# GpSimd normalises the next chunk's x before it begins the result's sum: two yacc buffers, and first gates asked for one pair later

## The reference, cut to what matters

```python
xn = layernorm(x)                                   # x: [2, 2048, 128]
# 1. a selective state space layer with N = 16 states per channel
dt = soft_clamp(softplus(xn @ Wdt.T + bdt), 0.001, 0.1, 0.5)
B, C = xn @ WB.T, xn @ WC.T                         # [b, l, 16] each
dA = exp(soft_clamp(dt * A, -8, 8, 0.5))
h = dA[t] * h + dt[t] * B[t] * xn[t]                # for every t, rescaled if its norm is over 20
y = sum_n h[:, n] * C[t, n] + Dp * xn[t]
# 2. a mixture of 64 experts (top 8 within the best 4 of 8 groups) and a shared expert
g = gates(xn @ router_w.T)                          # [tokens, 64], most of them 0
routed = sum_e g[:, e] * (relu(xn @ up[e])**2 @ down[e])
shared = relu(xn @ shared_up)**2 @ shared_down
out = x + y + routed + shared
```

## Time and profile before

| what | value |
|---|---|
| median of 3 runs | 568.28 us (566.95 to 568.99) |
| the profiled execution's own time | 569.49 us |
| its span in the profile | 567.7 us |
| busy share of the span | PE 90%, DVE 86%, ACT 83%, POOL 83% |
| TensorE clock, mean of the span | 0.994 of full |
| DMA | 149.32 MB, mean 263 GB/s |

### The profile page before, as it was taken

One profiled execution on the slowest core, in us unless ns is written; L12 is line 12 of the kernel. 1 busy time (PEld: TensorE's weight loads), 2 busy tenths in 40 slices (PEclk: granted clock), 3 DMA queues, 4 the chain that ended last, 5 costly groups with the idle time before them and its releaser, 6 DMA issues.

```text
span 567.7 us, 7918 instructions
## 1 busy us (share of the span) xinstructions
PE 508.1 (90%) x1666; PEld 279.1 (49%) x1666; DVE 485.4 (86%) x1150; ACT 468.6 (83%) x922; POOL 472.4 (83%) x438
## 2 busy tenths in 40 slices
PE   2148999999999989999999999989999999999996
PEld 1025545464555545555455545545455554555552
DVE  3647899889988899889998889889998899979993
ACT  2767799798987989888986999869998789978872
POOL 2399889897998979897998978989898979979762
PEclk9998999999999999999999999999999999999998
DMA  8946877897869877697678877697777976789951
GB/s 202 326 163 227 272 250 228 282 321 248 268 201 359 267 260 255 235 383 253 241 251 314 302 261 259 195 365 269 268 248 236 360 254 238 236 331 351 321 183 38
DMA packets 65649, 149.32 MB, mean 263 GB/s; under 512 B 14048, under 2 KB 31040, under 8 KB 65600
## 3 DMA queue, kind: packets, MB, share of 16 engines
q1 hardware_dynamic: 63728, 147.07, 77.0%
q10 hardware_dynamic: 1872, 1.75, 0.9%
HBM read 143.03 MB, written 5.77 MB: 262 GB/s over the span
## 4 chain that ended last, share of the span: by engine, by line
POOL 44%; issue 26%; PE 14%; DVE 13%; DMA 2%; POOLq 1%; ACT 0%; SPq 0%; DVEq 0%; ACTq 0%
POOL yacc L549 15%; POOL bc_rows L540 9%; PE DN L1087 7%; POOL xn L446 3%; DVE g L834 3%; DVE relu L884 3%; DVE bc_rows L896 2%; PE U L1037 2%; PE U L1038 2%; PE U L1039 2%; DVE DC L943 2%; POOL xt L453 2%; POOL rstd L440 1%; DMA bc_rows<-bc_dram 1%; POOL ot L521 1%
## 5 line engine op out<-in xcount | busy, mean ns | idle before, releaser
L1087 PE MATMUL DN<-act,down 128*128 128x512 f32 x512 | 262.3, 594 | 1.8 <-ACT act L718 1.8
L884 DVE SCALAR_TENSOR_TENSOR relu<-U,gate_rows 128x512 f32<-128x512 f32 x256 | 173.7, 678 | 36.2 <-PE U L1039 18.3
L718 ACT ACTIVATE act<-relu 128x512 f32<-128x512 f32 x272 | 169.1, 622 | 37.4 <-DVE relu L884 31.9
L549 POOL TENSOR_TENSOR yacc<-yacc,bc_rows 128x512 f32<-128x512 f32 x120 | 153.8, 1282 | 43.5 <-DVE bc_rows L896 43.5
L1037 PE MATMUL U<-x_hi,up_hi 128*128 128x512 f32 x256 | 164.0, 641 | 15.3 <-DVE relu L884 13.6
L540 POOL TENSOR_TENSOR bc_rows<-dtx_all,bc_rows 128x512 f32<-128x512 f32 x128 | 164.6, 1286 | 13.5 <-DMA bc_rows<-bc_dram 13.5
L943 DVE TENSOR_TENSOR_SCAN DC<-DC,carry,bc_rows 128x512 f32<-128x512 f32 x96 | 122.7, 1278 | 0.0
L1087 PEld LDWEIGHTS DN<-act,down 128*128 128x128 f32 x512 | 95.6, 189 | 28.8 <-ACT act L718 6.5
L1038 PE MATMUL U<-x_lo,up_hi 128*128 128x512 f32 x256 | 101.4, 396 | 0.0
L1039 PE MATMUL U<-x_hi,up_lo 128*128 128x512 f32 x256 | 101.0, 394 | 0.0
L1037 PEld LDWEIGHTS U<-x_hi,up_hi 128*128 128x128 f32 x256 | 48.3, 188 | 103.5 <-DVE relu L884 61.0
(11 more groups left out here) (113 smaller groups left out, 495.1 us busy)
## 6 DMA issues: line engine op xcount, KB each, us to landing
bc_rows<-bc_dram SPq DMA_DIRECT2D x128, 512.0 KB, 5.9
gate_rows<-gate_dram SPq DMA_DIRECT2D x128, 512.0 KB, 4.8
xs<-in_L_attn_x SPq DMA_DIRECT2D x8, 256.0 KB, 5.2
down<-in_L_ffn_down_w SPq DMA_DIRECT2D x8, 256.0 KB, 4.9
xr<-in_L_attn_x SPq DMA_DIRECT2D x8, 256.0 KB, 6.4
rest_kept_dram<-rest SPq DMA_DIRECT2D x8, 256.0 KB, 4.4
out<-res SPq DMA_DIRECT2D x8, 256.0 KB, 4.5
dtx_all<-in_L_ffn_up_w SPq DMA_DIRECT2D x3, 512.0 KB, 5.4
```

What stands on the lines that cost most here:

```text
L549: g.tensor_tensor(yacc[:, :], yacc[:, :], c_rows[:, (c * N + n) % BUFS, :], ALU.add).then_inc(yacc_done, 1)
L718: a.activation(act_at(c, slot), relu[:, slot % 2, :], ACT.Square).then_inc(sq_done, 1)
L884: v.scalar_tensor_tensor(out=relu[:, slot % 2, :], in0=U[slot % 2][:, :], scalar=0.0, in1=gate_rows[:, k // 2 % SBUFS, slot % 2, :], op0=A ...
L1087: mm(DN[:, :], w, act_at(c, slot), start=slot == 0, stop=slot == SLOTS - 1).then_inc(down_done, 1)
```

## The change

POOL takes the power and the normalised x one slot earlier (slots 0 and 1 where they were in 1 and 2). `out_begin` moves from slot 0 to slot 5. So that the next chunk may start its sum before the old one is read, `yacc` gets two halves, used by turns, and the first `ymul` of a chunk waits for the `out_begin` of two chunks ago. In SP's list each gate row stands one state later.

```diff
-        yacc = sb("yacc", [P, CT])
+        yacc = sb("yacc", [P, 2, CT])
...
                     rows(c, n)
-                    if n:
-                        gates_in(c, n - 1)
+                    if n > 1:
+                        gates_in(c, n - 2)
+                gates_in(c, N - 2)
                 gates_in(c, N - 1)
...
             def prep(pc, slot):
                 chain = chains["p"]
-                if slot == 1:
+                if slot == 0:
                     pool.wait_ge(var_ready, pc + 1)
...
-                if slot == 2 and pc:
+                if slot == 1 and pc:
                     pool.wait_ge(rstd_ready, pc + 1)
...
-                g.tensor_tensor(ot[:, :], rest[:, par(c)], yacc[:, :], ALU.add).then_inc(ot_begun, 1)
+                g.tensor_tensor(ot[:, :], rest[:, par(c)], yacc[:, c % 2, :], ALU.add).then_inc(ot_begun, 1)
...
-                    g.tensor_tensor(yacc[:, :], yacc[:, :], c_rows[:, (c * N + n) % BUFS, :], ALU.add).then_inc(yacc_done, 1)
+                    g.tensor_tensor(yacc[:, c % 2, :], yacc[:, c % 2, :], c_rows[:, (c * N + n) % BUFS, :], ALU.add).then_inc(yacc_done, 1)
...
                 for slot in range(SLOTS):
-                    if slot == 0 and not first:
+                    if slot == 5 and not first:
                         out_begin(c - 1)
...
                 if n == 0:
-                    wait(dve, ot_begun, c)
-                dst = c_rows[:, (c * N + n) % BUFS, :] if n else yacc[:, :]
+                    wait(dve, ot_begun, c - 1)
+                dst = c_rows[:, (c * N + n) % BUFS, :] if n else yacc[:, c % 2, :]
```

## The result

| | before | changed |
|---|---|---|
| median in one comparison | 568.63 us (566.95 to 569.59, 4 runs) | 561.07 us (560.99 to 561.15, 4 runs) |
| profiled execution's own time | 569.49 us | 560.99 us |
| span | 567.7 us | 559.2 us |

The ratio is 0.987 (95%: 0.9854 to 0.9885). The medians are 7.6 us apart; by the interval the gain lies between 6.5 and 8.3 us. The profiled executions are 8.5 apart, because the profiled one of the kernel before is 0.9 above the median. The forecast was 560.1, with -8.2. The spread shrank too, from 2.6 us to 0.2.

The account below looks back on a forecast made before the run. PE and DVE were taken to bound the kernel as a pair, neither catching up a stall. PE's `xn` stalls in chunks 1 to 6 (7.2 shown plus 0.96) gave -8.2, chunk 0 gave 0: 568.28 to 560.1 us, range 557 to 565.

Parts of the forecast that it names:

- POOL's order: POOL at a chunk's start: power waits 0.53 us for the variance, yet `xn` is done 2.46 us earlier, 1.67 before PE needs it.
- SP's order: SP's load queue: row 2 issued at 228.1 instead of 233.4, 5.3 us earlier, so POOL's 1.16 us wait for it goes.
- both parts are needed for the whole 2.46: At chunk starts: `xn` comes the full 2.46 us earlier only with POOL's new order and SP's new list together.
- it is what allows `ot` to be late: Two halves of `yacc`: worth nothing by themselves, but they let POOL do `ot` behind the first sum.
- the boundaries each 1.2 to 1.6 us closer together: Sign expected in the profile after: every chunk boundary closer to the next by this amount.
- Does DVE follow?: DVE after the transposes: its waits, at least 0.94 us, cover PE's 0.85 gain, so DVE starts its own stage earlier by that.
- rival 1: DVE's stage absorbs half: only its `x_lo` wait, 0.39 of 0.85, is regained; gain 3.8 us, 564.5 us; chance 0.18.
- rival 2: No change: PE is early at slot 4 and waits for DVE's relu instead; 568 us; chance 0.10.
- Chunk 0: PE's longest stall, 2.30 us, counted as 0 gain because DVE waits 1.60 us for POOL there; upper bound 2.5.
- rival 4: More gain: chunk 0 pays too, up to 2.5 us; 557.6 us; chance 0.08.
- The rule that speaks against it: DMA queues take turns, so row 2 may delay the gate store by 1.9 us, leaving gate row 0 0.3 us spare, not 2.2.
- Rival 3: Slower: gate row 0 comes later than its 2.19 us slack at seven boundaries and DVE stands still; +17, 585 us; chance 0.06.

Follow-up runs that it names:

- sp_only: Kernel before with only SP's new list, each gate row one state later: 560.82 us, ratio 0.9877.
- power_and_sp: Kernel before with power and `xn` one slot earlier and SP's new list, but one `yacc` and `ot` in slot 0: 561.10 us, ratio 0.9849.
- pool_only: Changed kernel with SP's old list, so POOL's new order and two halves of `yacc` only: 561.70 us, ratio 0.9893.
- power_early_only: Kernel before with only the power in slot 0 and `xn` in slot 1; one `yacc`, SP's old list: 561.31 us, ratio 0.9883.
- ot_late_only: Kernel before with only two halves of `yacc` and `ot` in slot 5: 570.79 us, ratio 1.0057.
- The split runs: Changed kernel with POOL's chunk 0 weight splittings moved to DVE: the first, 559.11 us; the first two, 561.44; those two with POOL held for the second, 557.99.
- the limits in batch 2: Changed kernel with gate rows four or five states after their own state's row, 581.44 and 669.30 us; or with `xn` in slot 4 behind the sum, 589.11.
- split_two_held: Changed kernel with the first two chunk 0 weight splittings on DVE and POOL waiting for the second before `xt`: 557.99 us, ratio 0.9792.
- split_two_on_dve: Changed kernel with the first two of POOL's three chunk 0 weight splittings done by DVE: 561.44 us, ratio 0.9857.

## Why the prediction was right, by its own steps

**The size.** -8.2 us forecast, -8.5 between the profiled executions, -7.6 between the medians. The kernel before scatters by 2.6 us here and by up to 6.4 in the batches; sp_only and power_and_sp, whose own times are 560.8 and 561.1, read as gains of 7.1 and 8.3 against it. So the medians do not tell 7.2 from 8.2. The chunks do: the rule that a stall is counted from the distance of the records' starts (0.86), and not from the idle time shown, gave 0.16 per chunk, and the gains of the table lie 0.14 to 0.22 us above the idle times shown in five of six chunks (0.38 in the sixth).

**POOL's order.** The new wait for the variance was forecast at 0.53 us for each boundary and is 0.76 at chunk 1, 0.7 on average: the path from DVE's aggregation to POOL's next start costs more than the end of its record says. It lies in the slack. That is 1.5 us at chunk 1. At the start of chunk 3, for which 1.67 was forecast, it is only 0.84 (`xn` done at 240.96, PE's transposes at 241.80), for a reason that the prediction does not have, the late row 0 of the next paragraph. The forecast time holds because there was more slack than needed.

**SP's order.** POOL's wait for row 2 is gone at every boundary. The one wait for a row that is left is for row 0 of chunk 3, two rows earlier in POOL's stream:

```profile
230.03 1.28 POOL L541 TENSOR_TENSOR bc_rows<-dtx_all,bc_rows 128x512 f32<-128x512 f32 x1 [1.28 <-DMA bc_rows<-bc_dram]
```

In SP's queue the three rows now stand ahead of the gate row that waits:

```profile
222.43 3.23 SPq L348 DMA_DIRECT2D bc_rows<-bc_dram  x3
231.71 0.53 SPq L361 DMA_DIRECT2D gate_rows<-gate_dram  x1
```

Row 2 is issued at 225.35, when its buffer is free, as forecast. But row 0 took 7.5 us from issue to landing here where it took 6.8 before, and row 2 took 7.4 where 5.8 was assumed. Over the span the median of the gate rows' landing rose from 4.8 to 5.6 us and that of the B and C rows fell from 5.9 to 5.5.

**The statement that was too strong** is "both parts are needed for the whole 2.46". It is true of the 2.46 us by which `xn` comes earlier, and it misleads as to time: PE lacked only 0.85 to 1.99, and pool_only, sp_only and power_early_only (561.70, 560.82 and 561.31 us) each come within 0.7 us of the changed kernel. With one of them the lateness is gone; the second adds slack that nobody uses. For the same reason "it is what allows `ot` to be late" was right, and the late `ot` was not needed; alone it gains nothing and is 2.9 us slower by the medians (ot_late_only).

**The statement that was wrong** is "the boundaries each 1.2 to 1.6 us closer together". The chunks became shorter by 0.83 to 2.05 us, each by its own stall, and the prediction itself had 0.85 for one of them. The sum was right, since it was taken from all the stalls.

**Does DVE follow?** Yes: each chunk is shorter by its stall, and rival 1 (564.5) and rival 2 (568) are out. The windows of the earlier trace rows could not have shown this: PE is busy in all 5.00 us of both, so they do not tell whose stage it is.

**Chunk 0.** The 0 was right, with the sign of the evidence as forecast (DVE's wait for `sfc` longer, 1.60 to 4.51), and rival 4 is out. The split runs show the reason by removing it.

**The rule that speaks against it.** The gate store at the same boundary after (ACT's queue, then the DMA issue with KB and us to landing), and DVE's first read of the gate row that waits for it, which SP issues at 231.71:

```profile
223.50 0.47 ACTq L676 DMA_DIRECT2D gate_dram<-gate  x1
```

```profile
gate_dram<-gate ACTq DMA_DIRECT2D x1, 128.0 KB, 8.1
```

```profile
237.13 0.68 DVE L885 SCALAR_TENSOR_TENSOR relu<-U,gate_rows 128x512 f32<-128x512 f32 x1
```

The store took 8.1 us where it took 6.4. At this boundary the 1.7 us more would fit the rule of the Trainium skill (DMA: Bandwidth & Descriptors, Queues, rings and completion order) that the queues take turns, and the 1.9 us of the row's traffic. But the seven stores for chunks 1 to 7 took 6.0, 7.0, 8.1, 6.6, 7.1, 5.9 and 5.2 us, where they took 5.8, 6.0, 6.4, 6.5, 7.4, 6.8 and 5.4: longer in four, shorter in three, and the median over all eight is 6.3 us where it was 6.2. So these runs do not show that row 2 delays the store. Gate row 0 landed at 235.9 and was read at 237.13, so 1.2 us of its slack of 2.2 were left. Rival 3 did not come; its place was right, but the limits in batch 2 show that I looked for its price at the boundaries alone, whereas gate rows that stand too far back are late at many states.

## What to carry to other kernels

A stall is worth what it takes the consumer to start when it could have, and no more: edits that shorten the same lateness do not add up, so try each alone and keep the smallest (here three lines in the order of the loads). A queue that issues in order delays everything behind its blocking wait (here row 2, by 5.3 us), so a transfer whose buffer is already free belongs in front of one that waits for a store, but only as far back as the delayed one's own slack allows, counted at every place and not only where one looks. Before work is given to an engine that waits, look at what the instruction in front of it waits for, and, for DVE beside POOL, at where its inputs lie.

## What the hardware showed that I had not expected

DVE and POOL excluded each other in both places where a split on DVE met POOL's stream. A `tensor_tensor` of DVE with both inputs in SBUF, started 0.07 us before a POOL instruction, took 1.24 us and POOL's took 2.28 instead of 1.29. The same DVE instruction, started at 47.93 in the middle of a gapless run of POOL instructions, took 5.25 us, until 1.08 us after the end of that run; in split_two_held it ended 1.11 us after the POOL instruction that ran when it started. The Trainium skill (SBUF — State Buffer, Who interferes with whom) says that a DVE instruction with two SBUF inputs contends with a GpSimd instruction that reads SBUF, over a shared read interface, and that the order of issue decides who is held up; the trace agrees with both. What this case adds is that the one held up was not let in between two instructions of the other: three more of POOL's (48.35, 49.62 and 50.85 us) started while it waited. Whether the sixth run of split_two_on_dve (557.65 us) is one in which DVE came first, was not seen in a profile.

The pause of 3.82 us before 67.09 us in chunk 0 was followed by a stretch of PE at the 1.2 GHz level (granted clock 0.52 in the window), while the time of the kernel did not show it, since PE was not the engine that set the pace there. In power_and_sp a pause of 4.10 us at the same place was followed by a window with 0.74, and in sp_only one of 1.52 us by a window at 1.00.
